# Sharing the low-part subtractions of two expert layers between VectorE and GpSimd, and drawing up the second layer's tile plan in another order

## The reference, cut to what matters

```
# layer 0: one expert of 8 for each row, at most 81 rows an expert here
slot = jnp.where(valid, top1 * capacity + rank, trash)
h = gelu(einsum('ecd,edf->ecf', eb, W1) + b1);  y = einsum('ecf,efd->ecd', h, W2) + b2
x = x + y[slot] * combine_w

# layer 1: two experts of 8 for each row, no limit
topv, topi = jax.lax.top_k(logits, 2);  gates = softmax(topv)
h = silu(x @ gate_w[e].T) * (x @ up_w[e].T);  acc += (h @ down_w[e].T) * w[e]
```

## Time and profile before

| | |
|---|---|
| median of 3 runs | 3956.62 us |
| the profiled execution, its own time | 3955.32 us |
| its span, first to last instruction | 3954.0 us |
| PE busy | 3667.2 us (93%) |
| DVE busy | 2522.7 us (64%) |
| ACT busy | 1894.5 us (48%) |
| POOL busy | 1744.6 us (44%) |
| granted TensorE clock, mean | 0.945 of 2.4 GHz |

### The profile page before, as it was taken

The page is one execution under the profiler, slowest core; times in us unless marked ns, Lnnn a source line. Parts: engine busy times, 40 slices in busy tenths (PEclk is TensorE's granted clock), DMA queues, the critical chain, the costliest instruction groups (busy, mean ns, idle before and its releaser), DMA issues. The chain is left out here.

```text
span 3954.0 us, 46465 instructions
## 1 busy us (share of the span) xinstructions
PE 3667.2 (93%) x18156; PEld 2357.4 (60%) x18156; DVE 2522.7 (64%) x3446; ACT 1894.5 (48%) x1950; POOL 1744.6 (44%) x760
## 2 busy tenths in 40 slices
PE   8999999699999999977796999999999887799997
PEld 6888888455555555432674455555554366588886
DVE  3222222287777777537695877777776465699997
ACT  2111111145555555632584455555555321577775
POOL 0110001048889989814000389999889320100000
PEclk9999999879999999986798699999999999799999
DMA  7444454613332333100697233333331100799996
GB/s 255 166 163 167 151 179 160 186 55 92 86 86 73 84 87 86 36 23 9 258 368 226 69 86 86 74 85 93 86 86 38 49 1 17 280 369 382 369 377 253
DMA packets 194890, 572.78 MB, mean 145 GB/s; under 512 B 23888, under 2 KB 89456, under 8 KB 143088
## 3 DMA queue, kind: packets, MB, share of 16 engines
q1 hardware_dynamic: 155888, 496.39, 38.5%
q10 hardware_dynamic: 36864, 67.13, 4.5%
q0 software_dynamic: 1920, 6.29, 0.5%
HBM read 449.66 MB, written 120.06 MB: 144 GB/s over the span
## 5 line engine op out<-in xcount | busy, mean ns | idle before, releaser
L615 DVE TENSOR_REDUCE maxima<-psum 128x1 f32<-128x512 f32 x2048 | 1287.9, 684 | 393.5 <-PE psum L486 390.1
L583 ACT ACTIVATE pt<-psum 128x1024 f32<-128x1024 f32 x1024 | 1016.1, 1026 | 751.7 <-PE psum L494 746.0
L597 POOL TENSOR_TENSOR exp_sums<-pt 128x1024 f32<-128x1024 f32 x342 | 818.3, 2393 | 394.7 <-ACT pt L583 249.8
L486 PE MATMUL psum<-ks,first_q 96*128 96x512 f32 x2048 | 815.6, 458 | 42.1 <-DMA first_q<-q_parts 42.0
L600 POOL TENSOR_TENSOR exp_sums<-exp_sums,pt 128x1024 f32<-128x1024 f32 x310 | 737.3, 2378 | 44.5
L486 PEld LDWEIGHTS psum<-ks,first_q 96*128 96x128 f32 x2048 | 401.3, 196 | 486.6 <-DVE maxima L615 344.4
L506 PE MATMUL psum<-pt,vs 128*32 128x512 f32 x4096 | 674.3, 598 | 4.0 <-DVE head_rows L625 2.4
L510 PE MATMUL psum<-exp_sums,constants 128*32 128x512 f32 x1408 | 670.1, 598 | 0.0
L494 PE MATMUL psum<-qs,ks 97*128 97x512 f32 x2048 | 647.8, 399 | 13.0 <-ACT pt L583 13.0
L1303 DVE TENSOR_TENSOR moe_cut<-moe_raw,moe_cut 128x2048 fp32r<-128x2048 f32 x244 | 557.3, 2291 | 56.6 <-ACT moe_cut L1245 51.6
L1245 ACT CAST moe_cut<-moe_raw 128x2048 fp32r<-128x2048 f32 x244 | 467.3, 1922 | 64.4 <-PE psum L97 64.2
(11 more groups left out here) (316 smaller groups left out, 4603.2 us busy)
## 6 DMA issues: line engine op xcount, KB each, us to landing
moe_raw<-in_moe_w SPq DMA_DIRECT2D x244, 1024.0 KB, 7.7
ks<-k_parts SPq DMA_DIRECT2D x384, 256.0 KB, 4.7
k_parts<-kparts ACTq DMA_DIRECT2D x256, 256.0 KB, 2.5
v_heads<-vrow SPq DMA_DIRECT2D x32, 1024.0 KB, 5.7
vs<-v_heads SPq DMA_DIRECT2D x32, 1024.0 KB, 5.3
cx<-in_ctx SPq DMA_DIRECT2D x16, 1024.0 KB, 8.9
first_q<-q_parts SPq DMA_DIRECT2D x96, 64.0 KB, 4.1
qs<-q_parts SPq DMA_DIRECT2D x96, 64.0 KB, 4.8
```

The lines of the kernel that those rows point to most:

```text
L486: pe.matmul(bank[b], self.first_q[s][:, t * P:(t + 1) * P], ks[s][0:3 * DH, keys:keys + CHUNK], start=True, stop=True).then_inc(*self.firs ...
L583: act.activation(self.pt[:, self.slot(h, b) + i:self.slot(h, b) + i + 2, :], self.c.psum[:, at:at + 2, :], ACT.Exp).then_inc(*self.exp.up())
L597: engine.tensor_tensor(to, self.pt[:, slot:slot + R, :], self.pt[:, slot + R:slot + 2 * R, :], ALU.add).then_inc(*signal.up())
L615: dve.tensor_reduce(self.maxima[:, h % 2, i % TT, i // TT:i // TT + 1], bank[b], X, ALU.max).then_inc(*self.first_read.up())
```

## The change

It touches only the expert stages, with these parts:

- GpSimd makes the low part of pieces 1, 4 and 7 of a tile in layer 0 and of pieces 1, 4, 7 and 10 in layer 1; VectorE skips them. The signal `low` becomes `low_dve` and `low_pool`, and whoever waited for a piece's low part waits for the right one (`low_done`).
- In layer 0 the hidden block is copied out of PSUM by VectorE in place of ScalarE; in layer 1 `yrow` is.
- In layer 1 the tiles are numbered without gaps: the tiles of expert 0, then those of expert 1, and so on, so that every tile's expert is known only from the plan. SP waits for that (`slot_made`) before its first weight load, and reads the expert for each tile.
- GpSimd waits for both choices of slots before the first of its indirect transfers; the plan makes `owner` before `row_of`.
- VectorE in layer 1, and TensorE in both layers, wait for the router's weights and bias ahead of the normalization, not behind it.

```
+BY_POOL_0, BY_POOL_1 = (1, 4, 7), (1, 4, 7, 10)
-MORE1 = TILES1 - EXPERTS
...
+        self.by_pool = BY_POOL_1 if self.two else BY_POOL_0
...
+        pe.wait_ge(*self.router_in.all())
         self.norm.on_pe(pe)
-        pe.wait_ge(*self.router_in.all())
...
+        dve.wait_ge(*self.router_in.all())
         self.norm.on_dve(dve)
-        dve.wait_ge(*self.router_in.all())
...
+        dve.tensor_scalar(need, router.count[:], 0.0, None, ALU.is_gt).then_inc(*plan.up())
+        for k in range(1, TT):
...
+        dve.tensor_tensor(self.owner[:], end[0:1, None, :].to_broadcast([1, TILES1, EXPERTS]),
+                          c.iota[0:1, 0:TILES1, None].to_broadcast([1, TILES1, EXPERTS]), ALU.is_le).then_inc(*plan.up())
...
+        dve.tensor_copy(self.owneri[:], self.ownerf[:]).then_inc(*self.slot_made.up())
         dve.tensor_copy(self.row_of[:, 0, :], slot1).then_inc(*self.rows_known.up())
...
+    def low_done(self, g):
+
+        by_pool = g % self.pieces in self.by_pool
+        nth = sum((v % self.pieces in self.by_pool) == by_pool for v in range(g + 1))
+        return (self.low_pool if by_pool else self.low_dve).at(nth)
...
-        if not self.two:
+        if self.two:
+            sp.wait_ge(*self.slot_made.at(1))
+        else:
             sp.dma_start(self.bias1[:], self.A["moe0_b1"].rearrange("(e p) f -> p e f", p=P)).then_inc(*self.bias1_in.up())
         for j in range(self.tiles):
-            if j == EXPERTS:
-                sp.wait_ge(*self.slot_made.at(1))
-            expert = sp.value_load(self.owneri[0:1, j - EXPERTS:j - EXPERTS + 1], min_val=0, max_val=EXPERTS - 1) if j >= EXPERTS else j
+            expert = sp.value_load(self.owneri[0:1, j:j + 1], min_val=0, max_val=EXPERTS - 1) if self.two else j
             for w in range(self.pieces):
                 g = j * self.pieces + w
                 if g >= self.RAW:
-                    sp.wait_ge(*self.low.at(g - self.RAW + 1))
+                    sp.wait_ge(*self.low_done(g - self.RAW))
...
+        pool.wait_ge(*self.rows_known.at(self.choices))
         for n in range(self.choices):
-            pool.wait_ge(*self.rows_known.at(n + 1))
             for t in range(TT):
                 pool.indirect_dma_start(self.S["x_slots"], bass.IndirectOffsetOnAxis(ap=self.row_of[:, n, t:t + 1], axis=0), self.norm.rows[:, t, :], None).then_inc(*self.x_sent.up())
+        for g in range(self.tiles * self.pieces):
+            if g % self.pieces in self.by_pool:
+                pool.wait_ge(*self.high.at(g + 1))
+                pool.tensor_tensor(self.cut[:, g % self.CUT, 1], self.raw[:, g % self.RAW], self.cut[:, g % self.CUT, 0].bitcast(F32), ALU.subtract).then_inc(*self.low_pool.up())
...
-                act.wait_ge(*self.used.at(j * self.pieces + fb + 1))
-                act.copy(part, bank[fb]).then_inc(*self.h_done.up())
...
-            if self.two:
-                if j > 1:
-                    act.wait_ge(*self.y_out[j % 2].at(j // 2))
-                act.wait_ge(*self.used.at((j + 1) * self.pieces))
-                act.copy(self.yrow[:, j % 2, :], bank[self.OUT_BANK]).then_inc(*self.y_done.up())
...
-            if g >= last_piece:
+            if g >= last_piece or g % self.pieces in self.by_pool:
                 return
             dve.wait_ge(*self.high.at(g + 1))
-            dve.tensor_tensor(self.cut[:, g % self.CUT, 1], self.raw[:, g % self.RAW], self.cut[:, g % self.CUT, 0].bitcast(F32), ALU.subtract).then_inc(*self.low.up())
+            dve.tensor_tensor(self.cut[:, g % self.CUT, 1], self.raw[:, g % self.RAW], self.cut[:, g % self.CUT, 0].bitcast(F32), ALU.subtract).then_inc(*self.low_dve.up())
...
+            else:
+                dve.wait_ge(*self.used.at(j * self.pieces + fb + 1))
+                dve.tensor_copy(part, bank[fb]).then_inc(*self.h_done.up())
...
-            if not self.two:
-                if j > 1:
-                    dve.wait_ge(*self.y_out[j % 2].at(j // 2))
-                dve.wait_ge(*self.used.at((j + 1) * self.pieces))
+            if j > 1:
+                dve.wait_ge(*self.y_out[j % 2].at(j // 2))
+            dve.wait_ge(*self.used.at((j + 1) * self.pieces))
+            if self.two:
+                dve.tensor_copy(self.yrow[:, j % 2, :], bank[self.OUT_BANK]).then_inc(*self.y_done.up())
+            else:
                 dve.wait_ge(*self.bias2_in[j % 2].at(j // 2 + 1))
                 dve.tensor_tensor(self.yrow[:, j % 2, :], bank[self.OUT_BANK], self.bias2[:, j % 2, :], ALU.add).then_inc(*self.y_done.up())
```

More of the change, by code:

```diff
@@ L989, in run @@
             self.zeroed, self.plan, self.exped, self.slot_made, self.rows_known = c.signals(st, "zeroed plan exped slot_made rows_known")
-            self.high, self.low = c.signals(st, "piece_high piece_low")
+            self.high, self.low_dve, self.low_pool = c.signals(st, "piece_high piece_low_dve piece_low_pool")
             self.x_turned, self.xg_high, self.xg_low = c.signals(st, "x_turned xg_high xg_low")
@@ L1082, in plan_top2_on_dve @@
         dve.tensor_tensor(w2, d, w1, ALU.mult).then_inc(*plan.up())
[L1083 to L1086, removed]
+        need, end, start, _ = (self.tile_of[:, k, :] for k in range(4))
+        dve.tensor_scalar(need, router.count[:], 0.0, None, ALU.is_gt).then_inc(*plan.up())
+        for k in range(1, TT):
+            dve.wait_ge(*plan.at(4 + k))
@@ L1087, in plan_top2_on_dve @@
             dve.scalar_tensor_tensor(need, router.count[:], float(k * P), need, ALU.is_gt, ALU.add).then_inc(*plan.up())
-        dve.wait_ge(*plan.at(3 + TT))
+        dve.wait_ge(*plan.at(4 + TT))
         dve.tensor_tensor_scan(end, c.ones[:, 0:EXPERTS], need, 0.0, ALU.mult, ALU.add).then_inc(*plan.up())
-        dve.tensor_scalar(own, c.iota[:, 0:EXPERTS], float(P), -1.0, ALU.mult, ALU.add).then_inc(*plan.up())
         dve.wait_ge(*plan.at(5 + TT))
-        dve.tensor_tensor(more, end, need, ALU.subtract).then_inc(*plan.up())
+        dve.tensor_tensor(start, end, need, ALU.subtract).then_inc(*plan.up())
@@ L1093, in plan_top2_on_dve @@
         dve.wait_ge(*plan.at(6 + TT))
-        dve.tensor_scalar(more, more, float(P), float((EXPERTS - 1) * P - 1), ALU.mult, ALU.add).then_inc(*plan.up())
+        dve.tensor_scalar(start, start, float(P), -1.0, ALU.mult, ALU.add).then_inc(*plan.up())
         dve.wait_ge(*plan.at(7 + TT))
-        dve.tensor_tensor(more, more, own, ALU.subtract).then_inc(*plan.up())
-        dve.tensor_scalar(prod[:], router.rank[:], float(P), None, ALU.is_gt).then_inc(*plan.up())
+        dve.tensor_tensor(self.chosen[:], router.rank[:], start[:, None, :].to_broadcast([P, TT, EXPERTS]), ALU.add).then_inc(*plan.up())
@@ L1098, in plan_top2_on_dve @@
+        dve.wait_ge(*plan.at(8 + TT))
+        dve.tensor_tensor(prod[:], router.hot[:, :, 0, :], self.chosen[:], ALU.mult).then_inc(*plan.up())
         dve.wait_ge(*plan.at(9 + TT))
-        dve.tensor_tensor(prod[:], prod[:], more[:, None, :].to_broadcast([P, TT, EXPERTS]), ALU.mult).then_inc(*plan.up())
-        dve.tensor_tensor(self.chosen[:], router.rank[:], own[:, None, :].to_broadcast([P, TT, EXPERTS]), ALU.add).then_inc(*plan.up())
+        dve.tensor_reduce(slot1, prod[:], X, ALU.add).then_inc(*plan.up())
@@ L1185, in into_hidden @@
         def into_hidden(j, g, to):
-            pe.wait_ge(*self.low.at(g + 1))
+            pe.wait_ge(*self.low_done(g))
             for k in range(KD):
@@ L1251, in leave_hidden @@
         def leave_hidden(j, fb):
-            part = self.h[:, fb * 512:(fb + 1) * 512]
             if self.two:
                 act.wait_ge(*self.used.at(j * self.pieces + 2 * fb + 1))
-                act.activation(part, bank[2 * (fb % 2)], ACT.Silu).then_inc(*self.silu.up())
-            else:
-                act.wait_ge(*self.used.at(j * self.pieces + fb + 1))
-                act.copy(part, bank[fb]).then_inc(*self.h_done.up())
+                act.activation(self.h[:, fb * 512:(fb + 1) * 512], bank[2 * (fb % 2)], ACT.Silu).then_inc(*self.silu.up())
         def leave_turned(j, fb):
```

28 lines of the change are left out of this document (9 added, 19 removed).

## The result

| | before | after |
|---|---|---|
| median, us (4 runs each, one chip) | 3956.91 | 4094.01 (4079.4 to 4101.9) |
| ratio to before, 95% interval | | 1.0342 [1.0325, 1.0358] |
| profiled execution: time, span | 3955.3, 3954.0 | 4091.75, 4090.4 |

What follows compares the result with a forecast made beforehand. PE was taken to bound both layers, with VectorE's and GpSimd's low parts excluding each other. 3955.3 + 98 (layer 1 tiles) + 48 (layer 0 tiles) + 8 (start) = 4109 us, range 4025 to 4155.

Steps and rivals of the forecast that it cites:

- What bounds: Both layers' tiles: PE sets the pace, at 25.8 us a tile in layer 0 and 35.2 in layer 1.
- The shared low parts: Tiles: VectorE's and GpSimd's low parts never overlap, so they sum to 36.8 us in layer 1, 29.7 in layer 0.
- More than the floor: Tiles: summed port time alone costs +55 us; waits behind VectorE's fixed order make it +98 in layer 1, +48 in layer 0.
- the term of layer 1: Layer 1's 15 tiles: each goes from 35.2 to 41.7 us, +98 us in all.
- The hand schedule: Tiles laid one after the other on a line: layer 1 settles at 41.7 us a tile, layer 0 at 31.8.
- rival 2: Tiles: PE's gaps also make the clock fall, +69 us at one fall a tile, 4178 us; above 4150, chance 0.11.
- Layer 0: Layer 0's 8 tiles: 31.8 us each instead of 25.8, PE losing 1.6, 0.5, 2.5 and 3.0; +48 us.
- The moved copies: VectorE's total of 25.1 us a layer 1 tile isn't the bound, ACT's relief is worth nothing; no separate cost.
- The start: Layer 1's start: bias wait +5.9, plan steps +0.4, sends -3, rows' load behind weights +5; together +8 us, between +3 and +13.
- 1 (4018): Tiles: only the shared port's total counts, 36.8 and 29.7 us a tile, +55 us; 4015 to 4060 us, chance 0.20.
- Rival 3: Tiles: low parts don't hinder each other; layer 0 gains up to 9.4 us, the start costs 8; 3954 us, chance 0.07.

Runs made afterwards that it cites:

- one-input run: Changed kernel with VectorE's low parts replaced by a sum over the raw piece, which reads one SBUF tensor: 4021.01 us, 1.0162.
- the split alone: Kernel before with only the low parts of pieces 1, 4, 7 (layer 0) and 1, 4, 7, 10 (layer 1) on GpSimd: 4069.15 us, 1.0293.
- the run without p7: Changed kernel with the low part of piece 7 in layer 0's tiles given back to VectorE: 4086.56 us, 1.0339.
- the experiment with an idle PE: Kernel before with PE made to wait once a tile of layer 1, ahead of piece 3, for three GpSimd memsets: 4041.46 us, 1.0221.
- the run with the start alone: Changed kernel with all low parts on VectorE and both copies back on ScalarE: 3965.99 us, 1.0026.
- the two edits that gained 20.8 us: Kernel before with next tile's rows loaded two pieces before a tile's end, and first three pieces cut during layer 1's plan: 3934.89 us, 0.9949.

## Why the prediction was right

**What bounds.** Confirmed: PE set the pace. In no run do the tiles average under 35.1 us in layer 1 or 24.3 in layer 0, and at these times PE is busy throughout.

**The shared low parts.** Confirmed: held operations end 2.15 us behind GpSimd's end in the tiles too. The one-input run narrows it: at 128 x 2048 the subtraction of two SBUF tensors is held and the reduce of one isn't. That is what the page quoted in the prediction ("SBUF — State Buffer" of the Trainium skill, same section) says of two inputs. But the number of inputs isn't all. L841 (one input, 0.43 us alone, 1.37 beside GpSimd) I had counted as the same, and layer 0's cast (one input, 0.42 alone, 3.93 beside GpSimd) is held too. Both take about 0.8 ns for each of their 512 columns, the reduce 1.1 for each of its 2048; whether that is what sets them apart I didn't test.

**More than the floor.** The direction and the mechanism held, the term of layer 1 was mis-sized: 41.7 us a tile forecast, 39.9 measured. The hand schedule had two stalls a tile, 3.6 at p3 and 3.1 at the turn. The runs show one: 3.0 at p3 in the changed kernel, and 1.7 to 3.6 at the turn in most tiles of the split alone, of the copies on ACT and of the run without p7. In its place stands what I had left to rival 2: the clock. By the windows, PE waits 46.1 us in 540, or 13.5 tiles: 3.4 a tile, and is busy 36.5 against 35.2: 1.3 more, at a mean clock of 0.97. Together 4.7; the experiment with an idle PE gives the same 4.7 from a wait of 2.95. The signs I had named say the same: 6 to 7 us idle a tile with PE busy 85% at clock 1.00 was forecast, 3.4 with 91% at 0.97 came.

**Layer 0**, forecast 31.8 (its terms add up to 32.0), measured 32.75, is nearly right for partly wrong reasons, which is luck. Of its 200 us (6.1 tiles) PE waits 36.5, 6.0 a tile, where I had 7.6, and is busy 26.8 a tile in place of 24.3 (150.6 us in 6.2 tiles): 2.5 by the clock of 0.91, for which I had nothing, and which is under the 0.95 that I had set as the sign of rival 2. The third turn waits up to 1.44 us (1.6 forecast), for moe_h; then comes one wait of 4.61 at p7, for the held cut of the turned block, where I had 2.5 at p6 and 3.0 at p7.

**The moved copies.** I put them into the sums without a price of their own. The run with them back on ACT is 8 to 10 us faster, nearly all of it in layer 1, where the pattern of waits changed without them in another run; their own price stays open.

**The start.** +8 forecast; +9.0 in the trace, +9.7 in the run with the start alone. The bias costs 6.35 where I had 5.9; the other terms 3.2 for an estimated 0.4 + 5 - 3. That they fit is partly luck: the plan and the sends gained 5.2 us, not 2.6 (the plan got 1.6 shorter, not 0.4 longer), and the weight loads beside the sends cost 8.4, not 5.

**The rivals.** 1 (4018) was too low: waits do stand beside the port. The run without p7 refutes it as a rule, as 27.4 us of port time by the same count (29.7 less one GpSimd part, plus one of VectorE's) still gave 32.6. Rival 2 was wrong as a case, right as a mechanism: the clock falls once a tile or so, for half of my 3 us in layer 1, and it isn't an alternative to the waits but their follower. Rival 3 fell with the first duration of 6.10 us. By stage the forecast was 28 us too high in layer 1's tiles, 7 too low in layer 0's, 1 too low at the start and 2 in all else: 18 over the profiled execution, 15 over the median.

The split costs 113 alone and the start 9.7 alone, 123 of 137. The rest, some 14 us (12 by all executions), comes with the copies or with the pattern in which the tiles settle; which of them stays open, as does what picks the pattern. Open as well is how much of layer 0's loss is clock and how much wait in the split alone, and why the clock differed between executions of the kernel with an idle PE.

## What to carry to other kernels

Before work is moved from VectorE to GpSimd, look at what both read from SBUF: VectorE's subtractions of two SBUF tensors, and layer 0's one-input cast as well, did not overlap with GpSimd's low parts but added to them (a reduce of one tensor, and all that took an operand from PSUM, did overlap), and the price is set by what is queued behind the held operation. Where TensorE is never idle, relieving another engine gains nothing; look for where TensorE waits and issue that transfer or that operation earlier, as the two edits that gained 20.8 us here do. A stall put into a full TensorE is to be priced with the slow products behind it: 3.0 us cost 4.7. And where such waits depend on a race, the same instructions can settle in two patterns, so a difference of 10 us between two kernels is put down to an edit only where the edited stage shows it.

## What was unexpected of the hardware

A GpSimd memset (128 x 2048, writes only) took 1.80 to 1.83 us beside low parts of VectorE, and held none of them (2.27 to 2.30). GpSimd's operations are held as well, 4.50 to 6.47 us, and where VectorE reads one tensor they stay within 4.50 to 5.18. At layer 1's start before, the issue of a send took 6.38 us beside three low parts; with those made earlier the same issues took 0.96 to 1.03. One part fewer on GpSimd in layer 0 left the tile at 32.6 us, from 32.75, since the wait moved. A load of 256 KB of rows took 9.4 us from issue to landing when issued behind three weight loads of 1 MB and 5.2 behind one.
